# Sixteen-head attentions of 8-wide heads: ScalarE subtracts the maximum of four heads inside its exponential, VectorE of twelve

## What is computed

```python
q = _split_heads(query @ Wq + bq, B)
k = _split_heads(key @ Wk + bk, B)
v = _split_heads(value @ Wv + bv, B)
scores = jnp.einsum('bhqd,bhkd->bhqk', q, k) * scale
scores = jnp.where(mask == 0, NEG_INF, scores)
probs = jax.nn.softmax(scores, axis=-1)
attn = jnp.einsum('bhqk,bhkd->bhqd', probs, v)
return attn.transpose(0, 2, 1, 3).reshape(B, -1, DIM_MODEL) @ Wo + bo
```

## Time and profile before

| | us |
|---|---|
| median of 3 runs (1315.12 to 1317.58) | 1316.79 |
| the profiled execution's own time | 1312.83 |
| its span in the trace | 1311.0 |
| mean granted TensorE clock, share of full | 0.948 |
| TensorE busy | 1142.2 |
| TensorE weight loads | 838.0 |
| VectorE busy | 765.1 |
| ScalarE busy | 682.4 |
| GpSimd busy | 364.4 |

### The profile page before, as it was taken

How to read it: one execution, slowest core, us unless ns; L and a number is a source line. 1 busy time by engine, 2 the same in 40 slices (tenths; PEclk the granted TensorE clock), 3 DMA queues, 4 the chain that set the end, 5 groups by cost and what they waited for, 6 DMA issues and landing times. The chain is left out here.

```text
span 1311.0 us, 24476 instructions
## 1 busy us (share of the span) xinstructions
PE 1142.2 (87%) x9697; PEld 838.0 (64%) x9697; DVE 765.1 (58%) x1671; ACT 682.4 (52%) x1205; POOL 364.4 (28%) x340
## 2 busy tenths in 40 slices
PE   1778898489999999999998599969439997999998
PEld 0567367478888888888885366643225664466667
DVE  5858535465656565656553379964537996722224
ACT  1677630165666666666654166656116665644441
POOL 3200001222222323232322422203662320744441
PEclk9999899699999999999999789989768997999999
DMA  4500000100000000000000000000000000000000
GB/s 166 189 1 1 0 1 1 65 1 1 1 1 1 1 1 1 1 2 1 1 2 1 0 2 2 2 1 0 0 0 2 2 2 2 1 0 8 9 0 17
DMA packets 6526, 16.27 MB, mean 12 GB/s; under 512 B 1312, under 2 KB 3568, under 8 KB 5520
## 3 DMA queue, kind: packets, MB, share of 16 engines
q1 hardware_dynamic: 6416, 14.74, 3.1%
HBM read 13.69 MB, written 1.05 MB: 11 GB/s over the span
## 5 line engine op out<-in xcount | busy, mean ns | idle before, releaser
L1099 POOL TENSOR_TENSOR work<-work 128x1024 f32<-128x1024 f32 x64 | 121.3, 1896 | 302.4 <-DVE work L1177 302.4
L1164 DVE TENSOR_REDUCE work<-psum 128x8 f32<-128x1024 f32 x64 | 78.0, 1219 | 93.0 <-PE psum L1000 93.0
L1116 ACT ACTIVATE work<-work 128x1024 f32<-128x1024 f32 x64 | 67.4, 1053 | 98.3 <-DVE work L1168 98.3
L1175 DVE TENSOR_REDUCE work<-work 128x8 f32<-128x1024 f32 x64 | 77.3, 1208 | 68.2 <-ACT work L1116 68.2
L1491 PEld LDWEIGHTS psum<-w_down,work 128*128 128x128 f32 x768 | 99.5, 191 | 24.4 <-issue 21.7
L887 ACT ACTIVATE work<-psum 128x512 f32<-128x512 f32 x128 | 72.8, 596 | 67.0 <-PE psum L777 66.1
L1491 PE MATMUL psum<-w_down,work 128*128 128x128 f32 x768 | 100.6, 275 | 0.7 <-DVE x L1576 0.7
L1568 DVE TENSOR_TENSOR work<-psum,big 128x512 f32<-128x512 f32 x67 | 45.8, 688 | 87.5 <-PE psum L1471 85.5
L919 DVE TENSOR_REDUCE work<-psum 128x8 f32<-128x1024 f32 x64 | 75.4, 1219 | 32.9 <-PE psum L765 18.8
L777 PEld LDWEIGHTS psum<-ident,work 128*128 128x128 f32 x512 | 57.4, 143 | 43.9 <-issue 30.7
L1168 DVE TENSOR_TENSOR work<-psum,work 128x1024 f32<-128x1024 f32 x64 | 78.4, 1225 | 6.4
(11 more groups left out here) (319 smaller groups left out, 2544.5 us busy)
## 6 DMA issues: line engine op xcount, KB each, us to landing
x<-in_x SPq DMA_DIRECT2D x1, 1024.0 KB, 4.8
ctx_tok<-in_ctx SPq DMA_DIRECT2D x1, 1024.0 KB, 6.8
ctxt<-in_ctxt SPq DMA_DIRECT2D x1, 1024.0 KB, 10.3
mask<-in_mask SPq DMA_DIRECT2D x1, 1024.0 KB, 6.5
w_down<-in_down SPq DMA_DIRECT2D x1, 1024.0 KB, 7.0
ctx_tok<-in_g SPq DMA_DIRECT2D x1, 1024.0 KB, 4.9
big<-in_u SPq DMA_DIRECT2D x1, 1024.0 KB, 6.9
out<-x SPq DMA_DIRECT2D x4, 256.0 KB, 2.2
```

The costliest lines, as they stand in the source:

```text
L1099: pool.tensor_tensor(prob[:, u % 2, h, :], prob[:, u % 2, h, :], rinv[:, u % 2, h].unsqueeze(2).broadcast_to([P, 8, P]), ALU.mult)\
L1116: act.activation(p, p, ACT.Exp).then_inc(S["exp"], 1)
L1164: dve.tensor_reduce(nmax[:, u % 2, h], s, AX.X, ALU.max, negate=True).then_inc(S["max"], 1)
L1175: dve.tensor_reduce(rsum[:, u % 2, h], prob[:, u % 2, h, :], AX.X, ALU.add).then_inc(S["sum"], 1)
```

## The change

In each batch the first twelve heads go as before: VectorE subtracts, in pieces of 1024 and 512 columns, and ScalarE takes the exponential in place, in the same pieces. For the last four heads, which are bank 3, ScalarE reads the scores from PSUM itself, one instruction a head (128 columns), with the head's negated maximum as the bias of the exponential. There are now three counts of `exp` a batch. The mask matmul into bank 3 of the next batch waits for all three, `turn` waits by the new counts, and VectorE waits for the exponentials of batch b-2 before it writes `nmax`.

```diff
--- before.py
+++ after.py
@@ -754,6 +754,8 @@
                     if b:
                         pe.wait_ge(S["sub"], 2 * b - 1 + half)
                     for g in (2 * half, 2 * half + 1):
+                        if b and g == 3:
+                            pe.wait_ge(S["exp"], 3 * b)
                         lhs, rhs = mask_rows(b)
                         pe.matmul(bank[g][:, :].rearrange("p (i c) -> p i c", i=4), lhs,
                                   rhs.unsqueeze(1).broadcast_to([rhs.shape[0], 4, P]),
@@ -768,8 +770,8 @@
 
             def turn(b, g):
                 n = 4 * b + g
-                if g % 2 == 0:
-                    pe.wait_ge(S["exp"], 2 * b + g // 2 + 1)
+                if g != 1:
+                    pe.wait_ge(S["exp"], 3 * b + max(g, 1))
                 if n >= 2:
                     pe.wait_ge(S["pt"], n - 1)
                 for i in range(4):
@@ -878,10 +880,14 @@
                 act.wait_ge(S["proj"], n + 1)
                 evict(0, n, src)
             for b in range(NB):
-                for half in range(2):
+                for half, width in enumerate((1024, 512)):
                     act.wait_ge(S["sub"], 2 * b + half + 1)
-                    p = prob[:, b % 2, half * 1024:(half + 1) * 1024]
+                    p = prob[:, b % 2, half * 1024:half * 1024 + width]
                     act.activation(p, p, ACT.Exp).then_inc(S["exp"], 1)
+                for h in range(12, 16):
+                    ins = act.activation(prob[:, b % 2, h * P:(h + 1) * P], bank[3][:, (h - 12) * P:(h - 11) * P],
+                                         ACT.Exp, bias=nmax[:, b % 2, h:h + 1])
+                ins.then_inc(S["exp"], 1)
                 for g in range(4):
                     act.wait_ge(S["turn"], 4 * b + g + 1)
                     act.activation(probt[:, g, :], bank[4 + g % 2][:, :], ACT.Copy).then_inc(S["pt"], 1)
@@ -914,19 +920,21 @@
             dve.wait_ge(S["xb"], 1)
             for b in range(NB):
                 dve.wait_ge(S["score"], b + 1)
+                if b >= 2:
+                    dve.wait_ge(S["exp"], 3 * (b - 1))
                 for half in range(2):
                     s = psum[:, 2 * half:2 * half + 2, :].rearrange("p n (i c) -> p (n i) c", i=4)
                     dve.tensor_reduce(nmax[:, b % 2, 8 * half:8 * half + 8], s, AX.X, ALU.max, negate=True)\
                        .then_inc(S["max"], 1)
                 if b >= 2:
                     dve.wait_ge(S["turn"], 4 * (b - 1))
-                for half in range(2):
-                    s = psum[:, 2 * half:2 * half + 2, :].rearrange("p n (i c) -> p (n i) c", i=4)
+                for half, n in enumerate((8, 4)):
+                    s = psum[:, 2 * half:2 * half + n // 4, :].rearrange("p n (i c) -> p (n i) c", i=4)
                     dve.wait_ge(S["max"], 2 * b + half + 1)
-                    dve.tensor_tensor(prob[:, b % 2, half * 1024:(half + 1) * 1024]
+                    dve.tensor_tensor(prob[:, b % 2, half * 1024:half * 1024 + n * P]
                                       .rearrange("p (h c) -> p h c", c=P), s,
-                                      nmax[:, b % 2, 8 * half:8 * half + 8].unsqueeze(2)
-                                      .broadcast_to([P, 8, P]), ALU.add).then_inc(S["sub"], 1)
+                                      nmax[:, b % 2, 8 * half:8 * half + n].unsqueeze(2)
+                                      .broadcast_to([P, n, P]), ALU.add).then_inc(S["sub"], 1)
                 if b >= 2:
                     residual_of(b - 2)
                 if b >= 1:
```

## The result

The changed kernel takes 1342.51 us (median of 4 runs, 1341.04 to 1345.56), the one before 1316.59 us in the runs beside it: a ratio of 1.0201, 95% interval 1.0178 to 1.0224, so 26 us slower. Its profiled execution has a span of 1343.8 us, 32.8 above the 1311.0 of before.

The account below looks back on a forecast made before the run. The prediction took a loop through TensorE's new wait for ScalarE's exponentials as the bound: +0.85 us in nine periods, +1.24 in six, 0.4 at the end, 15.5 a stage, 30.9 for two, on 1316.79: 1347.7 us, range 1333 to 1362.

Parts of the forecast that it names:

- The mechanism: In both stages, the new bank-3 mask wait puts ScalarE's exponentials on the loop: +1.24 us without a projection, +0.85 with one.
- the loop through L926: In batches without a projection, VectorE's subtraction releases TensorE's mask matmuls, then scores and the next reduction follow: 6.58 us.
- rival (a): The ScalarE chain hides and VectorE bounds: 12 of 30 periods lose 0.525 us each, 6.3 in all, 1310.5 us; chance 2%.
- The chain's terms: Pieces of the new loop, reduction, subtraction, exponentials, mask, scores, reduction: 7.82 us without a projection, against 6.58.
- scores to reduction: From the start of TensorE's score matmuls to VectorE's first reduction: 1.20 us.
- two reductions: VectorE's two reductions, from the start of the first to the subtraction: 2.28 us.
- to the first exponential: From the subtraction's start on VectorE to ScalarE's first exponential, without a projection: 1.24 us.
- exponentials: On ScalarE, from the first exponential's start to the last one's end: 0.94 + 0.48 + 1.14 = 2.56 us.
- semaphore: Delay from the end of ScalarE's last exponential to TensorE's released mask matmul: 0.10 us.
- mask to scores: On TensorE, from the bank-3 mask matmul to the score matmuls: 0.44 us, bounds 0.25 and 0.70.
- The first two periods: The first one or two periods run at a lower clock, 0.76 from 758 to 765 us, but were costed like the rest.
- Rival (c): The waits lower TensorE's clock; at 0.76 throughout both stages, 65 us more, 1382 us; chance 5%.

Follow-up runs that it names:

- the first experiment: The changed kernel with its four small exponentials moved ahead of the 1024-column one and the bank-3 mask matmul waiting only for them: 1316.71 us, ratio 1.0006.

## Why the prediction was right, and where it was off

**The mechanism** held: faster was given 3%, and the measured 1342.51 lies in 1333 to 1362, below the 1347.7. The stages cost 27.3 us by the trace where 30.9 were forecast; by the medians it is 25.9, and this last difference is in parts that the change doesn't touch.

**What bounds the kernel.** I wrote that without a projection "VectorE's own work and the loop through L926 are both tight". The loop was: it closes at 6.57, yet TensorE's release by L926 at 814.60 cost nothing, since the same 6.58 stands in the first experiment with no such wait. VectorE's own work is 6.50, the period with TensorE's path shortened, and TensorE's path is 6.58. Had I added up TensorE's part (5.61 to the masks in the earlier trace rows, and 0.97 from masks to scores in the earlier trace rows, where nothing is waited for) I would have had it: rival (a), whose 6.3 us of gain assumed VectorE as the bound, was too generous even in its own terms; the whole work taken away gave 1.3 us (0 to 2.6), and no steady period became shorter by it.

**The chain's terms**, period without a projection, predicted and measured: scores to reduction 1.20 and 1.21; two reductions 2.28 and 2.27; to the first exponential 1.24 and 1.24; exponentials 2.56 and 2.61 (825.39 to 828.00); semaphore 0.10 and 0.05; mask to scores 0.44 and 0.32. Sum 7.82 and 7.70, so +1.12 for the +1.24. The exponentials took 0.05 more than predicted and the semaphore 0.05 less; that these cancel is luck. The 0.12 is the last term: I took it as two mask matmuls less one, but behind a mask matmul that waits alone the scores' weights load after 0.23 us of idle time, and behind a run of four after 0.42. With a projection the mean is 8.06, +0.79 for +0.85.

**The small exponentials** were 366 ns, four in 1.12 us, where I had 1.14 from L484's row. The Trainium skill's estimate for an activation with a pointer bias (page "ScalarE: Activation LUTs", section "What ACT_TABLE_LOAD costs") gave 1.27 and was too high by 0.15; the Trainium skill's figure for ScalarE in the section "The TRN2 errata" of "VectorE: DVE Perf Modes" gave an estimate of 1.0 and was too low by 0.12. That section of the Trainium skill advises against many small tiles for instructions that read SBUF. These read PSUM, and here too one wide exponential took less time than four small ones, 0.67 us against 1.12. The exponential of 512 columns takes 617 ns; the step I took for it, 0.48, was a little short (1.49 us from the first exponential's start to the first small one's, where I had 1.42).

**The first two periods** were costed like the rest, +1.24 and +0.85 a stage; they cost +1.4 together in the first stage (16.54 to 17.96), as the kernel before was slow there too: its second period took 8.74 us at a granted clock of 0.82. The 13 steady periods cost 11.9 for 13.0, the ends 0.4 for 0.4. Per stage that is 13.7 for 15.5.

**Nothing outside the two stages changes** was true of the work and not of the time: the stretch between the stages took up to 6.0 us more in other kernels, and the part behind the second one up to 2.3 less. In the changed kernel both happened to take what they took before (106.6 and 208.3 us). That the total came out so near the stages' own sum is luck to that extent. Rival (c), a lower clock inside the stages, didn't come: 1.00 over the 13 steady periods, with gaps of 0.55 to 0.95 us between matmuls in each.

## What to carry to other kernels

When work moves to another engine, look at what holds its input buffer and until when: here ScalarE became the last reader of a PSUM bank and read it behind 1.5 us of other work, and one wait on one bank stopped the queue of the engine that bounds the kernel. Let the reader that frees a contended buffer go first, and let the writer wait for exactly that count. Sum each engine's own path before calling one the bound: an engine without idle time can be the second of two nearly equal ones, and freeing it gives nothing until the first is shortened.

## What the runs showed of the hardware that I had not expected

The clock granted to untouched code can depend, reproducibly, on the code ahead of it: three profiles with the same first stage of 104.6 to 104.7 us had 112.5 us in an untouched stretch of 106.5, at a clock of 0.60 in its first 21.5 us in place of 0.91. Over all profiles the stretch took 106.5 to 112.5 us, and what decides it is not known. Here a gain of 3.0 us in a stage came back as a loss of 2.4 in the whole, so a change of 0.2 to 0.3% is judged by its own stage in the trace as well as by the total.
